# Recurrence of a hybrid kernel: the two squares that feed the sum of squares, one moved to ScalarE, one doubled there

## The reference, cut to what matters

```python
def step(h, inp):
    x_t, dt_t, B_t, C_t, xr_t = inp
    h_carrier = h.mean(axis=1)
    T = jnp.cos((c_phase(xr_t) - c_phase(h_carrier)) / 2.0) ** 2
    alpha = jnp.exp(dt_t[..., None] * A_neg)
    expo = 1.0 + (1.0 - alpha) * KAPPA * (1.0 - T[:, None, :])
    mag, ph = (c_mag(h), c_phase(h))
    cmag = jnp.minimum(jnp.exp(expo * jnp.log(mag + 1e-08)), 10.0)
    h = from_polar(cmag, ph)
    Bx = B_t[:, None, :, :] * (dt_t * x_t)[:, :, None, None]
    h = h + Bx
    h = from_polar(jnp.tanh(c_mag(h)), c_phase(h))
    y_t = jnp.einsum('bnc,bdnc->bd', C_t, h)
    return (h, y_t)
```

## Time and profile before

| | us |
|---|---|
| median of 3 runs | 12653.35 |
| lowest and highest run | 12646.96, 12656.97 |
| the profiled execution, its own time | 12647.4 |
| its span in the trace | 12645.5 |
| DVE busy in the span | 10103.6 |
| ACT busy in the span | 8436.4 |
| PE busy in the span | 10574.1 |

### The profile page before, as it was taken

How to read it: one execution, slowest core, us unless ns; L and a number is a source line. 1 busy time by engine, 2 the same in 40 slices (tenths; PEclk the granted TensorE clock), 3 DMA queues, 4 the chain that set the end, 5 groups by cost and what they waited for, 6 DMA issues and landing times. The chain is left out here.

```text
span 12645.5 us, 256282 instructions
## 1 busy us (share of the span) xinstructions
PE 10574.1 (84%) x68398; PEld 5344.3 (42%) x68414; DVE 10103.6 (80%) x56587; ACT 8436.4 (67%) x42451; POOL 94.9 (1%) x165
## 2 busy tenths in 40 slices
PE   6888888888888888888888888888888977898998
PEld 5333333333333333333333333333344546653335
DVE  5888888888888888888888888888874948868875
ACT  6777777777777777777777777777754722264666
POOL 0000000000000000000000000000000100000000
PEclk8666766766676667667666766766678988998999
DMA  2000100001000100001000100001000000011100
GB/s 57 15 15 15 21 15 15 15 18 18 15 15 15 21 15 15 15 15 21 15 15 15 22 15 15 15 15 21 15 11 12 1 24 6 7 36 45 29 24 22
DMA packets 339594, 229.62 MB, mean 18 GB/s; under 512 B 27662, under 2 KB 324184, under 8 KB 337885
## 3 DMA queue, kind: packets, MB, share of 16 engines
q1 hardware_dynamic: 338140, 213.30, 8.0%
HBM read 187.41 MB, written 25.43 MB: 17 GB/s over the span
## 5 line engine op out<-in xcount | busy, mean ns | idle before, releaser
L548 PE MATMUL scan_p_car<-scan_warm 128*128 128x448 bf16 x15872 | 5429.8, 488 | 1007.6 <-DVE scan_state_ps L674 998.6
L548 PEld LDWEIGHTS scan_p_car<-scan_warm 128*128 128x128 bf16 x15872 | 1505.7, 116 | 3689.3 <-DVE scan_state_ps L674 2101.6
L595 ACT ACTIVATE scan_act_ps<-scan_state_ps 128x64 f32<-128x64 f32 x2048 | 426.0, 208 | 1865.2 <-DVE scan_state_ps L674 1865.2
L595 ACT ACTIVATE scan_act_ps<-scan_act_ps 128x64 f32<-128x64 f32 (+1 forms) x8193 | 1610.7, 197 | 65.5
L677 DVE SCALAR_TENSOR_TENSOR scan_uw<-scan_w,scan_rsq 128x64 f32<-128x64 f32 x2048 | 461.3, 225 | 857.9 <-ACT scan_rsq L595 857.9
L536 PEld LDWEIGHTS scan_p_car<-scan_hs,scan_mean_mat 32*32 32x32 f32 x16392 | 371.4, 124 | 1811.9 <-DVE scan_hb L677 1799.2
L541 PE MATMUL scan_p_car<-scan_eps_row,ones 1*128 1x3 f32 x4102 | 1015.9, 315 | 39.1 <-DMA scan_a_log<-L_attn_a_A_log 38.9
L570 PE MATMUL scan_p_y<-scan_c_masked,scan_hb 128*64 128x4 f32 x16384 | 1030.5, 228 | 0.0
L536 PE MATMUL scan_p_car<-scan_hs,scan_mean_mat 32*32 32x2 f32 x16392 | 547.6, 191 | 564.4 <-DVE scan_hb L677 542.0
L674 DVE TENSOR_TENSOR scan_c<-scan_V,scan_power_ps 128x64 f32<-128x64 f32 x4096 | 722.3, 217 | 242.3 <-ACT scan_power_ps L595 18.5
L541 PEld LDWEIGHTS scan_p_car<-scan_eps_row,ones 1*128 1x128 f32 x4102 | 837.9, 254 | 72.0 <-DMA scan_a_log<-L_attn_a_A_log 39.3
(11 more groups left out here) (453 smaller groups left out, 18338.8 us busy)
## 6 DMA issues: line engine op xcount, KB each, us to landing
scan_step_in<-scan_scratch SPq DMA_DIRECT2D x520, 256.0 KB, 6.2
qk_scratch<-qkv_parts SPq DMA_DIRECT2D x32, 384.0 KB, 2.5
attn_qT<-qk_scratch SPq DMA_DIRECT2D x192, 64.0 KB, 2.2
attn_kT<-qk_scratch SPq DMA_DIRECT2D x192, 64.0 KB, 2.2
scan_scratch<-prep_dts SPq DMA_DIRECT2D x32, 256.0 KB, 2.1
x<-L_attn_a_x SPq DMA_DIRECT2D x1, 4096.0 KB
out<-x SPq DMA_DIRECT2D x1, 4096.0 KB
filter_in_taps<-c_kT SPq DMA_DIRECT2D x1, 2048.0 KB
```

The costliest lines, as they stand in the source:

```text
L548: nc.tensor.matmul(p_car[slot][:, 64:512], warm[:, 0:P], warm[:, 64:512], start=True, stop=True)
L595: nc.scalar.activation(dst, src, func, **kw).then_inc(counts[par]["act"], 1)
```

## The change

ScalarE gets two more operations at the head of its step, ahead of the wait for `r2`. `nq` is the square of `w0 + EPS_PHASE` (the guard goes in as the bias of the activation) and waits for `w0`; `sq1` is the square of `w1`, waits for `w1`, and is written to the third slice of the PSUM tensor `power_ps`. VectorE loses its own `sq1` and loses `na`; it keeps `sq0` in a tile of its own. `r2` now waits for two counters, VectorE's (`sq0`) and ScalarE's (`sq1`), and reads one operand from PSUM. `n2` adds `nq` and `sq1` and has no wait of its own. The bias of the Ln that reads `n2` drops its `EPS_PHASE**2`, which is now inside `nq`.

```diff
-DVE_STEP = ["c0", "c1", "w0", "w1", "sq0", "sq1", "na", "r2", "n2", "bx0", "bx1", "uw0", "uw1", "h0", "h1", "nh", "hp", "Vm", "dot", "dl", "s", "V"]
-ACT_STEP = ["al", "l", "M", "ln2", "E", "rsq", "L1", "R", "th2", "l2", "mag", "nsq", "lm", "lnn", "lnh", "rs", "ru", "cm"]
+DVE_STEP = ["c0", "c1", "w0", "w1", "sq0", "r2", "n2", "bx0", "bx1", "uw0", "uw1", "h0", "h1", "nh", "hp", "Vm", "dot", "dl", "s", "V"]
+ACT_STEP = ["al", "nq", "sq1", "l", "M", "ln2", "E", "rsq", "L1", "R", "th2", "l2", "mag", "nsq", "lm", "lnn", "lnh", "rs", "ru", "cm"]
...
-        c, w, sq, uw, bx, Vm, V = (ph.sb(n, [P, 2, J]) for n in ("c", "w", "sq", "uw", "bx", "Vm", "V"))
-        na, rsq, R, th2, mag, ru = (ph.sb(n, [P, J]) for n in ("na", "rsq", "R", "th2", "mag", "ru"))
+        c, w, uw, bx, Vm, V = (ph.sb(n, [P, 2, J]) for n in ("c", "w", "uw", "bx", "Vm", "V"))
+        sq0, nq, rsq, R, th2, mag, ru = (ph.sb(n, [P, J]) for n in ("sq0", "nq", "rsq", "R", "th2", "mag", "ru"))
...
-        lm, cm = (power_ps[:, q * J:(q + 1) * J] for q in range(2))
+        lm, cm, sq1 = (power_ps[:, q * J:(q + 1) * J] for q in range(3))
...
+                            after(act, "dve", "w0", par, k)
+                            op(par, nq[:, :], w[:, 0, :], ACT.Square, bias=EPS_PHASE)
+                            after(act, "dve", "w1", par, k)
+                            op(par, sq1[:, :], w[:, 1, :], ACT.Square)
                             after(act, "dve", "r2", par, k)
                             op(par, lr[:, :], r2[:, :], ACT.Ln, bias=EPS_MAG)
                             after(act, "act", "l", par, k)
                             op(par, M[:, :], lr[:, :], ACT.Exp, scale=0.5)
                             after(act, "dve", "n2", par, k)
-                            op(par, ln2[:, :], n2[:, :], ACT.Ln, scale=SHIFT * SHIFT, bias=SHIFT * SHIFT * (EPS_PHASE * EPS_PHASE + 1e-24))
+                            op(par, ln2[:, :], n2[:, :], ACT.Ln, scale=SHIFT * SHIFT, bias=SHIFT * SHIFT * 1e-24)
...
-                            for comp in range(2):
-                                after(dve, "dve", f"w{comp}", par, k)
-                                tt(sem, sq[:, comp, :], w[:, comp, :], w[:, comp, :], ALU.mult)
+                            after(dve, "dve", "w0", par, k)
+                            tt(sem, sq0[:, :], w[:, 0, :], w[:, 0, :], ALU.mult)
                             after(dve, "dve", "sq0", par, k)
-                            stt(sem, na[:, :], w[:, 0, :], 2 * EPS_PHASE, sq[:, 0, :], ALU.mult, ALU.add)
-                            after(dve, "dve", "sq1", par, k)
-                            tt(sem, r2[:, :], sq[:, 0, :], sq[:, 1, :], ALU.add)
-                            after(dve, "dve", "na", par, k)
-                            tt(sem, n2[:, :], na[:, :], sq[:, 1, :], ALU.add)
+                            after(dve, "act", "sq1", par, k)
+                            tt(sem, r2[:, :], sq0[:, :], sq1[:, :], ALU.add)
+                            tt(sem, n2[:, :], nq[:, :], sq1[:, :], ALU.add)
```

## The result

The changed kernel takes 12761.37 us, median of 4 runs (12758.12 to 12774.06), against 12650.15 us before (4 runs): a ratio of 1.0088, with a 95% interval from 1.0074 to 1.0103. It is 111 us slower, 0.054 us for each of the 2048 steps. The forecast was 12642 us, in a range that ended at 12688.

A forecast was written before the change was run, and what follows sets the result against it. The recurrence bounds the kernel, decided by when `r2` ends. `r2`'s 7 ns a step (-14 us) and late instructions (+3) took the profiled 12647.4 us to 12636; runs' median 6 above: 12642, range 12600 to 12688.

The forecast's parts named there:

- step 4: Handover from ScalarE's `sq1` to VectorE's `r2`: 0.03 us, so `r2` begins at 0.937 against 0.945 before.
- The terms of ScalarE: Squares ahead of `r2`: `nq` at 0.52, `sq1` 0.15 behind it, lasting 0.236 and ending at 0.905 us.
- the 11 of the sum: Whole kernel: -14 us from `r2` and +3 from late instructions, -11 us in all.
- rival B: ScalarE's squares: `sq1` not held up by `nq`, as short as `l2`, or one of these; both give 12596 us; chance 0.25.
- B's case of a short `sq1` alone: At `r2`: only `sq1`'s duration is short, so `r2` begins at 0.928, 17 ns early and 3 longer; 12627 us.
- the 0.27 us: VectorE ahead of `r2`: two operations of 0.135 us leave, but turn into 0.26 us of waiting for ScalarE.
- the 553 us: VectorE ahead of `r2`: 0.27 us earlier over 2048 steps, the number the diff suggests, not what is gained.
- Rival C: ScalarE's squares: a Square reading SBUF costs more than Ln; `r2` at 0.974, 12722 us; chance 0.16.
- PE's clock: On PE: named as a reason if `r2` keeps its time but the mean step is off by over 10 ns.
- Late instructions: VectorE starts late in some steps though nobody is late; hangs on the place in the program; +3 us.
- 6 and 5 us in the bounds: Upper bound of the time: late instructions at 6 us and their shift at 5, within +48 us at worst.

The follow-up runs named there:

- e1: The changed kernel with the two waits of `r2` in the other order, ScalarE's `sq1` first, then VectorE's `sq0`: 12622.97 us against 12657.38, ratio 0.9974.
- e2: The kernel before with the two waits ahead of `c0` swapped, so the late `cm` is in the semaphore instruction: 12793.76 us against 12657.38, ratio 1.0109.
- e9: e8 with the two waits ahead of `r2` swapped, so the semaphore instruction holds VectorE's own square: 12770.58 us against 12675.89 for the kernel before, ratio 1.0076.
- e7: The kernel before with `r2` ahead of `na` on VectorE and nothing moved to ScalarE: 12701.02 us against 12657.71, ratio 1.0034.
- e4: The changed kernel with `r2`'s waits turned, `sq1` ahead of `nq` on ScalarE, and `n2` waiting for `nq`: 12601.35 us against 12657.38, ratio 0.9956.
- e8: The changed kernel with the squares exchanged, ScalarE squaring `w0` and VectorE `w1`, ScalarE's wait in the semaphore instruction: 12624.58 us against 12675.89 before, ratio 0.9959.
- e5: The kernel before with only the square of `w1` moved to ScalarE, `na` staying on VectorE: 12622.3 us against 12657.71, ratio 0.9971.
- e3: The changed kernel with `r2` adding `nq` in place of `sq0` and waiting for `sq1` alone: 12616.39 us against 12657.38 for the kernel before, ratio 0.9969.

## Why the prediction was wrong

- **The step that failed: step 4, the handover from ScalarE to VectorE, put at 0.03 us.** The 0.03 came from `uw0`, which has a single wait. `r2` has two, and the late one is in the semaphore instruction, where the handover takes 0.10: `sq1` ends at 0.90 and `r2` starts at 1.00. e1 takes the 0.07 away, e2 and e9 put it elsewhere. 0.07 x 2048 = 143 us is more than the whole difference between forecast and result, 119 us. The forecast added 3 us for instructions that arrive late, and did not ask which of the two waits the semaphore instruction holds. The order of the two names at `r2` stood in the listing ahead of the prediction; that `c0`, where ScalarE is the late one too and the handover is 0.03, has them the opposite way round, did not.
- **The terms of ScalarE came out nearly right, in part by luck.** `nq` started at 0.52, as forecast. `sq1`'s turn was 0.15 in the forecast and 0.163 in the trace, its duration 0.236 and 0.210. The two errors have opposite signs, and its end came at 0.894 instead of 0.905. With the handover of 0.03 restored (e1), `r2` is at 0.926, where step 4 had 0.937. These 0.011 us are 23 us in 2048 steps, the difference between the 34 us that e1 gains and the 11 of the sum. A duration below 0.23 was named as a sign of rival B, and B's case of a short `sq1` alone (`r2` at 0.928) is the one that e1 fits.
- **The reading of what the 0.27 us were worth was right, and its reason can be made sharper.** It is not only ScalarE that holds `r2`. e7 shows VectorE alone couldn't start `r2` before 0.93 either: `na` stood in a gap between `sq1` and the operation that needs it. Of the 553 us, the most there was to get with all on VectorE is what moves `r2` from 0.946 to 0.929 (the medians), about 35 us; e4 and e8 gain 0.4% with `r2` at 0.917.
- **Rival C had the sign and not the mechanism.** It said that a long Square on ScalarE makes `r2` late at 0.974. `nq` did last 0.256, as `th2` does, and its turn of 0.163 was close to C's 0.167; but `sq1` was short and ended early. No rival had the order of the waits, which is worth a rival of its own whenever an operation gets a second wait.
- **That the multiplications moved to ScalarE** is not what made this slower: with the waits turned, two squares on ScalarE beat the kernel before (e1, ratio 0.9974). What the runs show is the price of the semaphore instruction when the wait in it is the late one, 0.07 us here.
- **What is left of the loss.** By the medians over all steps `r2` starts 0.050 us later than before, it lasts 0.003 us longer (229 ns instead of 226), and 0.001 comes behind it; the step is 0.054 us longer. PE's clock is not the cause: the granted clock is 0.756 before and 0.748 after, but from the start of `h1` to ScalarE's reading of the product for the mean there are 0.631 and 0.633 us (medians).
- **Late instructions.** No run shows the terms of 3 us in the sum and of 6 and 5 us in the bounds. What the runs showed in their place: in the changed kernel `r2` starts at least 0.03 us behind its usual handover in 8 steps, 2.9 us in all. Taken together the long steps hardly moved: those that are over 0.06 us longer than the median exceed it by 55.2 us in sum before and 56.5 after. The median step of the kernel before is 4.437 us, 0.016 under the mean. In its trace 393 operations of the recurrence on VectorE start over 0.06 us later behind the operation before them than the median for their place in the step; the commonest distance between two of them (96 of 392) is 128 instructions of VectorE. That such starts come from fetching instructions is not shown; no run changed the fetching alone.

The fastest version is e4, the change with the late wait in the operation and the square that `r2` needs first: 0.9956 of the kernel before, and by the ratios some 167 us under the change as made. e8 is level with it.

## What to carry to other kernels

When an operation has two waits, find out which one becomes an instruction of its own, and give that place to the wait that ends first; write the late wait so that it goes into the operation. Here the order of two lines was worth 1.1% of the time, more than the moved work brought in any version. And before counting an operation's turn as a gain, look whether it fills the time in which its follower waits for an operand anyway: an operation that needs the one right before it starts 0.035 us after its end (`r2` in e7, `na` in e5), and so 0.25 us after its start, not after a turn of 0.135.

## What the runs showed of the hardware that was not expected

- A semaphore instruction that holds the late wait costs about 0.07 us on VectorE, for counters of ScalarE (the change against e1, e2) and of VectorE itself (e9 against e8). The operation starts 0.066 us after the start of that instruction in each of these traces; one that is over early costs nothing measurable (e3 against e1: ratios 0.9969 and 0.9974, with overlapping intervals).
- The second of two Squares on ScalarE is the shorter one: behind `nq`, `sq1` takes 0.21 us, and ahead of it 0.23; `nq` takes 0.26 when first and 0.24 when second. The distance of their starts is 0.163 in both orders, so they overlap by 256 less 163, 93 ns, in one order, and by only 228 less 163, 65 ns, in the other (the change, and e4).
- The same edit of one pair of lines is worth nothing that can be measured at `nh`, which is off the path, and 144 us at `r2`.
